# One scan loop over all 64 tiles: the next image's attention and first front inside the seventh tile

## The chip, the cores and the metric

One core of a Trainium2 chip runs the kernel. The metric is device time in microseconds (us) of one execution; the time before is the median of three runs.

## The reference, cut to what matters

The input `x` has 8 images of 512 channels and 64 x 64 positions. For each image two residual layers follow each other:

```
x = x + attention(_gn(x))      # group norm over 32 groups; Q, K from 4x4 means, V summed over 16 positions
x = x + ssm(_gn(x))            # group norm again, with moments of the new x
# attention: A = softmax(Q K^T / sqrt(512)), 256 x 256; out = repeat(A @ Vsum, 16)
# ssm: LayerNorm over 512 channels, cut in 4 chunks of 128; for each chunk
#   xi, z = in_proj; xc = silu(conv4(xi)); dt, B, C = x_proj(xc); dt = softplus(...)
#   h[t] = exp(dt*A) * h[t-1] + dt*xc*B   for 16 states and 256 inner channels;   y = sum over states of h*C
#   y = (y + xc*D) * silu(z); out_proj; + skip
# LayerNorm over 512 channels, 512 x 512 projection
```

The scan runs over all 4096 positions of an image, so its states and the convolution's last three columns go from tile to tile and start at zero in each image. The attention's output is needed before any position of the image can enter the second layer, and the second group norm needs the moments of the sum of both.

## The kernel before

An image is cut into 8 tiles of 512 positions (`T`), a tile into 4 **items** (one for each 128-channel chunk), an item into 16 **steps** (one for each state). A step is two scans on VectorE (DVE), one for each half of the 256 inner channels (`scan`, L921), with the decay `exp(dt*A)` written to PSUM by ScalarE (ACT, L649), the input product `u = dt*x*B` on DVE (11 of 16 steps, L901, `AHEAD` says in which step each is made) or on GpSimd (POOL, the 5 steps of `POOL_U`, L1187), the product with C on POOL (L1200) and the sum over states by an identity matmul on TensorE (PE, `state_sum`, L369). U, H and G are rings of four steps, so no engine can run more than four steps ahead of the one that frees a slot.

All five engines carry an order written out by hand. `window(tile, w)` emits the 16 steps of item `w` of a tile and, at fixed steps `s` in it, the **front** of item `w + 1`: the convolution as matmuls, its silu, the rows of B and C (stored and broadcast back by DMA from SyncE's queue, SP), and dt's softplus, which passes ACT, DVE (`dt_poly`, L938) and POOL (`dt_first`, `dt_sum`, `dt_x`, L1205 to L1214). `gate` (L927, step 2) waits until the state sums of the item before are complete. `j = w % 4` chooses what else lies in an item: the second LayerNorm of the tile before (j = 0), its projection and `finish` (j = 1, L957), the first LayerNorm of the next tile (j = 2) and the statistics of one slice of the *next image* (j = 3, `slice_moments`, `slice_rows`, `slice_blocks`). `late(j)` is 1 for j = 3 and moves the front one step back. The inner loop covers items 2 to 29 of an image as w = 2 to 5 of seven iterations.

Around it each image has a part of its own. On every engine `attention(b)` and `first_front` come first, alone, using the scan's own buffers (RING, ITEM, LV, LS, and DA, DTP, YP in PSUM); then windows 0 and 1, the loop, windows 2 and 3 of the last tile without a further front, and `last_end`, which ends the last tile.

## Time and profile before

| | |
|---|---|
| median of 3 runs | 17287.28 us (17285.9 to 17292.63) |
| the profiled execution's own time | 17281.15 us |
| its span, first to last instruction | 17279.2 us |
| DVE / POOL / PE / ACT busy, share of the span | 87% / 87% / 84% / 65% |
| mean granted TensorE clock | 0.931 |

The profile is of one execution; every row has its times. "Idle before, releaser" is the time an engine sat idle before a group of instructions and what ended it. In the 40 slices each digit is a busy share in tenths.

### The profile page before, as it was taken

What the parts mean: (1) busy time and instruction counts of PE and PEld (TensorE: products, weight loads), DVE (VectorE), ACT (ScalarE), POOL (GpSimd) and SP (SyncE); (2) the same over time, 40 slices, a digit from 0 to 9 for tenths busy, and PEclk for the clock granted to TensorE, in tenths of its full rate; (3) what the DMA queues carried; (4) which work ended last, traced back from release to release, by engine and by line L of the source; (5) the groups of instructions that cost most, each with busy time, mean ns of one, the idle gap of its engine ahead of it and who ended that gap; (6) DMA issues with size and microseconds to landing.
All of it is one profiled execution on the core that took longest, in us unless ns stands there. A gap on an engine that the chain in (4) does not pass through costs nothing. (4 is left out here: it accounts for less than half of the span.)

```text
span 17279.2 us, 159098 instructions
## 1 busy us (share of the span) xinstructions
PE 14535.6 (84%) x30720; PEld 5796.6 (34%) x30720; DVE 14988.9 (87%) x13132; ACT 11261.9 (65%) x18548; POOL 14970.7 (87%) x6268
## 2 busy tenths in 40 slices
PE   6888878888788887888878888788887888878888
PEld 2333333333333333333333333333333333333333
DVE  7999969999699996999969999699996999869998
ACT  4667657676566765667656666566665666656675
POOL 5999969999699996999969999699986999869998
PEclk8999989999899998999989999899998999989999
DMA  3444434444344443444434444344443444434443
GB/s 130 155 156 160 156 108 156 154 159 157 111 154 156 158 154 115 155 154 158 152 116 157 152 157 156 114 154 156 156 154 118 157 153 154 151 118 152 152 152 135
DMA packets 739059, 2535.91 MB, mean 147 GB/s; under 512 B 77240, under 2 KB 78016, under 8 KB 721728
## 3 DMA queue, kind: packets, MB, share of 16 engines
q1 hardware_dynamic: 738112, 2527.45, 42.8%
q14 instruction: 861, 7.05, 0.1%
q8 instruction: 86, 1.41, 0.0%
HBM read 2376.15 MB, written 150.99 MB: 146 GB/s over the span
## 5 line engine op out<-in xcount | busy, mean ns | idle before, releaser
L1200 POOL TENSOR_TENSOR RING<-RING,CS 128x1024 f32<-128x1024 f32 x4096 | 9832.9, 2419 | 1054.6 <-DVE RING L921 1037.3
L921 DVE TENSOR_TENSOR_SCAN RING<-DA,HS,RING 128x512 f32<-128x512 f32 x8192 | 9948.9, 1264 | 785.1 <-ACT DA L649 528.7
L369 PE MATMUL YP<-RING,EYE 128*128 128x512 f32 x16384 | 8378.6, 643 | 1931.3 <-POOL RING L1200 1899.3
L649 ACT ACTIVATE DA<-ITEM,AN 128x512 f32<-128x512 f32 x8192 | 5526.7, 685 | 3369.3 <-DVE RING L921 3359.7
L369 PEld LDWEIGHTS YP<-RING,EYE 128*128 128x128 f32 x16384 | 3122.7, 199 | 6731.5 <-issue 3495.4
L901 DVE TENSOR_TENSOR RING<-DTP,BS 128x1024 f32<-128x1024 f32 x2816 | 3374.9, 1206 | 0.2 <-DMA BS<-bc_rows 0.2
L1187 POOL TENSOR_TENSOR RING<-ITEM,BS 128x1024 f32<-128x1024 f32 x1280 | 3019.4, 2360 | 8.6
L369 PE MATMUL FL<-XN,WC 128*128 128x512 f32 x4096 | 1954.3, 622 | 48.1 <-ACT XN L734 36.6
L1205 POOL TENSOR_TENSOR ITEM<-ITEM,EX 128x1024 f32<-128x1024 f32 x256 | 602.6, 2354 | 1048.7 <-ACT EX L703 1048.7
L369 PEld LDWEIGHTS FL<-XN,WC 128*128 128x128 f32 x4096 | 847.4, 207 | 1194.5 <-issue 1151.3
L662 ACT ACTIVATE ITEM<-FL,COL 128x512 f32<-128x512 f32 x512 | 347.9, 680 | 1202.1 <-PE FL L369 1202.1
L369 PE MATMUL FL<-LS,WP 128*128 128x512 f32 x2048 | 978.4, 605 | 48.8 <-POOL LS L1218 48.8
L658 ACT ACTIVATE HS<-RING 128x2 f32<-128x2 f32 x4096 | 780.2, 190 | 12.3 <-DVE RING L921 12.3
L927 DVE TENSOR_TENSOR YZ<-ITEM,YP 128x1024 f32<-128x1024 f32 x256 | 311.0, 1215 | 535.6 <-PE YP L369 535.6
L369 PE MATMUL FL<-LS,MEAN 128*128 128x512 f32 x1024 | 561.7, 680 | 234.3 <-ACT LS L744 234.3
L938 DVE SCALAR_TENSOR_TENSOR YZ<-YZ,EM 128x1024 f32<-128x1024 f32 x256 | 519.8, 2030 | 233.8 <-ACT YZ L710 233.8
L369 PE MATMUL FL<-ROWS,WDT 8*128 8x512 f32 x1024 | 582.3, 648 | 50.5 <-ACT ROWS L675 15.9
L1210 POOL TENSOR_TENSOR ITEM<-ITEM,YZ 128x1024 f32<-128x1024 f32 x256 | 601.9, 2351 | 5.5 <-DVE YZ L938 4.9
L1214 POOL TENSOR_TENSOR ITEM<-ITEM 128x1024 f32<-128x1024 f32 x256 | 602.4, 2353 | 0.6
L369 PE MATMUL FL<-XN,WZ 128*128 128x512 f32 x1024 | 495.6, 606 | 126.9 <-ACT ITEM L662 126.9
L369 PEld LDWEIGHTS FL<-LS,WP 128*128 128x128 f32 x2048 | 391.2, 194 | 568.4 <-issue 567.5
L369 PE MATMUL FL<-YZ,WO 128*128 128x512 f32 x1024 | 507.0, 617 | 10.5 <-DVE YZ L927 10.5
(122 smaller groups left out, 10420.8 us busy)
## 6 DMA issues: line engine op xcount, KB each, us to landing
BS<-bc_rows SPq DMA_DIRECT2D x2048, 512.0 KB, 4.9
CS<-bc_rows SPq DMA_DIRECT2D x2048, 512.0 KB, 3.6
XR<-in_x SPq DMA_DIRECT2D x128, 1024.0 KB, 7.4
x_slices<-XR SPq DMA_DIRECT2D x64, 1024.0 KB, 8.0
XR<-x_slices SPq DMA_DIRECT2D x64, 1024.0 KB, 7.4
out<-XR SPq DMA_DIRECT2D x64, 1024.0 KB, 7.9
ITEM<-in_wqkv SPq DMA_DIRECT2D x24, 1024.0 KB, 5.5
bc_rows<-ROWS SPq DMA_DIRECT2D x256, 64.0 KB, 4.5
```

The source lines that it names most:

```text
L369: return pe.matmul(*a, **k)
L649: act.activation(DA[:, h, :], DT[:, i % 2, h, :], ACT.Exp, scale=AN[:, h, s:s + 1]).then_inc(dA_ready, 1)
L658: act.activation(HS[:, i % ITEMS, :, s:s + 1], H[:, slot(n), :, T - 1:T], ACT.Copy).then_inc(state_kept, 1)
L662: act.activation(XC[:, i % 2, h, :], FL[:, h, :], ACT.Identity, bias=CB[:, h:h + 1]).then_inc(xi_copied, 1)
L901: dve.tensor_tensor(U[:, slot(n)], DTP[:, :, :], BS[:, s % B_ROWS, :].unsqueeze(1).broadcast_to([P, NH, T]), ALU.mult).then_inc(u_dve, 1)
L921: dve.tensor_tensor_scan(H[:, slot(n), h, :], DA[:, h, :], U[:, slot(n), h, :], HS[:, i % ITEMS, h, s:s + 1], ALU.mult, ALU.add).then_inc( ...
L938: dve.scalar_tensor_tensor(out=YZ[:, :, :], in0=YZ[:, :, :], scalar=13.0 / 16, in1=EM[:, :, :], op0=ALU.add, op1=ALU.mult).then_inc(poly_r ...
L1187: pool.tensor_tensor(U[:, slot(n)], DTX[:, :, :], BS[:, s % B_ROWS, :].unsqueeze(1).broadcast_to([P, NH, T]), ALU.mult).then_inc(u_pool, 1)
L1200: pool.tensor_tensor(G[:, slot(n)], H[:, slot(n)], CS[:, s % C_ROWS, :].unsqueeze(1).broadcast_to([P, NH, T]), ALU.mult).then_inc(g_ready, 1)
L1205: pool.tensor_tensor(DT[:, i % 2], DT[:, i % 2], EX[:, :, :], ALU.add).then_inc(dt_begun, 1)
L1210: pool.tensor_tensor(DT[:, i % 2], DT[:, i % 2], YZ[:, :, :], ALU.add).then_inc(dt_ready, 1)
L1214: pool.tensor_tensor(DTX[:, :, :], DT[:, i % 2], XC[:, i % 2], ALU.mult).then_inc(dtx_ready, 1)
```

## The change

The image's own part goes. After one attention, one first front and windows 0 and 1 for image 0, one chain of windows runs through all 64 tiles. What image b + 1 needs is cut into pieces, and each piece has a step of a window of image b:

- Slices of statistics: one in w3 of tiles 0 to 3, two (w3 and w5) in tiles 4 and 5, none in tiles 6 and 7.
- In tile 6 (`coming=b + 1`): w2 has `aggregate`, the first group mean and variance; w3 the pooled inputs, the queries, keys and half of the values; w4 the other half, the scores and the exponentials; w5 the turned weights, the output O, its moments and the covariance. Projection 2 and 3 of w5 move back by up to one step.
- In w2 of tile 7 (`new=True`): the second variance, rstd and shift, and the front and first LayerNorm, one step later than elsewhere; its end (halo and first chunk) is in step 0 of w3 (`shifted`). ACT writes zeros in place of the kept states (`kept=False`) and of the halo.
- The results pass through the two front banks of PSUM (FP, LP) alone; Q, K, V and the weights A have buffers of their own; Wq and Wv are loaded into XT, Wk into XE, by SP's queue between its B and C rows. The norm of the pooled inputs moves from DVE to ACT (`pooled`, `summed`); the covariance is taken of the normed sums and divided back. In the beginning these loads come behind the statistics instead of ahead of them.

The diff, cut to its core (the pieces on the engines are the same operations as in the old `attention`, in halves):

```diff
+        QK = sb("QK", [P, 2, NCH, NB])
+        VS = sb("VS", [P, 2, CH])
+        AT = sb("AT", [P, 2, NB])
...
+        Q, K = QK[:, 0], QK[:, 1]
...
+        wt_flat, we_flat = (x.rearrange("p k t -> p (k t)") for x in (XT, XE))
+        WT, WE = (x.rearrange("p (k n) -> p k n", k=NCH) for x in (wt_flat, we_flat))
...
+            def load_wq(a):
+                sp.wait_ge(stats_done, a * NT + NT)
+                load_w(WT, 0, wq_loaded)
+            def load_wk(tile):
+                sp.wait_ge(stored, tile * 16)
+                load_w(WE, 1, wk_loaded)
+            def load_wv(a):
+                sp.wait_ge(q_ps, a * 2 + 2)
+                load_w(WT, 2, wv_loaded)
+            def load_end_after(t, tile, a):
+                sp.wait_ge(k_ps, a * 2 + 2)
...
+                if more:
+                    tile_step(b, 6, at, after_store=(b, 5), front=(b + 1, 0),
+                              extra={2: {0: lambda: load_wq(b + 1)},
+                                     3: {0: lambda: load_wk(at), 5: lambda: load_wv(b + 1)},
+                                     4: {1: lambda: load_end_after(6, at, b + 1)}})
+                    tile_step(b, 7, at + 1, after_store=(b, 6), front=(b + 1, 1))
...
+                    if new and s == 0:
+                        group_var(coming, 2)
...
+                            if new:
+                                pe.wait_ge(glog_ready, coming * 2 + 2)
+                            if j == 3 and coming is not None:
+                                pe.wait_ge(glog_ready, coming * 2 + 1)
...
+                        else:
+                            if s == 12:
+                                pe.wait_ge(final_ready, (ahead - 1) * NCH + 2)
+                                proj(2, (0, 1), low=True)
+                            if s == 13:
+                                proj(2, (2, 3), low=True)
+                            if s == 14:
+                                pe.wait_ge(final_ready, (ahead - 1) * NCH + 3)
+                                proj(3, (0, 1))
...
+                    if coming is not None and not new:
+                        if j == 2:
+                            if s == 9:
+                                front_left(tile, w + 1)
+                                group_mean(coming, 1)
+                            if s == 12:
+                                group_var(coming, 1)
+                        if j == 3:
+                            if s == 8:
+                                pe.wait_ge(yb_ready, tile * ITEMS + w)
+                                queries(coming, 0)
+                            if s == 9:
+                                front_left(tile, w + 1)
+                                queries(coming, 1)
+                            if s == 12:
+                                keys(coming, 0)
+                            if s == 13:
+                                keys(coming, 1)
+                            if s == 14:
+                                values(coming, 0)
+                            if s == 15:
+                                pe.wait_ge(k_ready, coming * 2 + 2)
+                        if j == 0:
+                            if s == 8:
+                                front_left(tile, w + 1)
+                                values(coming, 1)
+                            if s == 11:
+                                scores(coming)
+                            if s == 15:
+                                pe.wait_ge(prob_exp, coming + 1)
+                        if j == 1:
+                            if s == 8:
+                                front_left(tile, w + 1)
+                                turn(coming)
+                            if s == 10:
+                                attend(coming, 0)
+                            if s == 12:
+                                attend(coming, 1)
+                            if s == 15:
+                                group_mean(coming, 2)
...
+            with pe.Fori(0, BATCH - 1) as b:
+                with pe.Fori(0, NT - 2) as t:
                     for w in range(2, 2 + ITEMS):
                         window(b * NT + t, w)
-                window(b * NT + (NT - 1), 2, ln1=False)
-                window(b * NT + (NT - 1), 3, ln1=False, front=False)
-                last_end(b * NT + (NT - 1))
+                for w in range(2, 2 + ITEMS):
+                    window(b * NT + (NT - 2), w, coming=b + 1)
+                window(b * NT + (NT - 1), 2, new=True, coming=b + 1)
+                for w in range(3, 2 + ITEMS):
...
+            def keep_halo(new=False):
+                src = ZERO.unsqueeze(1).broadcast_to([P, NCH, HALO]) if new else XN[:, :, T:T + HALO]
...
+                    if coming is not None:
+                        if j == 1:
+                            if s == 0:
+                                prob_scale(coming)
+                            if s == 9:
+                                prob_turned(coming)
+                            if s == 11:
+                                attended(coming, 0)
+                            if s == 13:
+                                attended(coming, 1)
+                        if j == 2 and not new:
+                            if s == 14:
+                                group_rstd(coming, 1)
+                        if j == 2 and new and s == 1:
+                            group_rstd(coming, 2)
+                        if j == 3:
+                            if s == 2:
+                                pooled(coming)
+                            if s == 7:
+                                summed(coming)
+                            if s == 11:
+                                head(Q, BQ, q_ps, q_ready, coming, 0)
+                            if s == 12:
+                                head(Q, BQ, q_ps, q_ready, coming, 1)
+                            if s == 13:
+                                head(K, BK, k_ps, k_ready, coming, 0)
+                            if s == 15:
+                                head(K, BK, k_ps, k_ready, coming, 1)
+                        if j == 0:
+                            if s == 0:
+                                value_copy(coming, 0)
+                            if s == 10:
+                                value_copy(coming, 1)
+                            if s == 14:
+                                prob(coming)
...
+            def summed(a):
+                act.wait_ge(coef_ready, a * 2 + 2)
+                for k in range(NCH):
+                    last = act.activation(XS[:, k], XS[:, k], ACT.Identity, bias=GSH16[:, k:k + 1],
+                                          scale=GRS[:, k:k + 1])
+                last.then_inc(xs_norm, 1)
...
+                    if coming is not None:
+                        if j == 2 and not new:
+                            if s == 5:
+                                aggregate(coming)
+                            if s == 11:
+                                deviation(coming, 1)
+                            if s == 15:
+                                first_shift(coming)
+                        if j == 0:
+                            if s == 13:
+                                score_max(coming)
+                            if s == 15:
+                                score_sum(coming)
+                        if j == 1:
+                            if s == 12:
+                                o_moments(coming, 0)
+                            if s == 14:
+                                o_moments(coming, 1)
+                            if s == 15:
+                                covariance(coming)
+                        if j == 2 and new:
+                            if s == 0:
+                                deviation(coming, 2)
+                            if s == 2:
+                                second_shift(coming)
...
+            def deviation(a, n):
+                mean, var, first = (GMS[:, :], MV[:, :, 1], 1) if n == 1 else (M1[:, :], V1[:, :], 7)
+                dve.wait_ge(gmean_ready, a * 2 + n)
+                dve.tensor_copy(GMN[:, :], FP[:, 0:NCH]).then_inc(gmean_kept, 1)
+                dve.wait_ge(gmean_kept, a * 2 + n)
+                dve.tensor_tensor(DEV[:, :], mean, GMN[:, :], ALU.subtract).then_inc(chain, 1)
+                link(a, first + 1)
+                dve.tensor_tensor(GSQ[:, :], DEV[:, :], DEV[:, :], ALU.mult).then_inc(chain, 1)
+                link(a, first + 2)
+                dve.tensor_tensor(GVAR[:, :], GSQ[:, :], var, ALU.add).then_inc(dev_ready, 1)
+            def first_shift(a):
+                dve.wait_ge(grstd_ready, a * 2 + 1)
+                dve.tensor_scalar(GRS16[:, :], GRS[:, :], 1.0 / SS, None, ALU.mult).then_inc(coef_ready, 1)
+                dve.scalar_tensor_tensor(out=GSH[:, :], in0=GMN[:, :], scalar=-1.0, in1=GRS[:, :],
+                                         op0=ALU.mult, op1=ALU.mult).then_inc(gshift_ready, 1)
...
+            def covariance(a):
+                dve.wait_ge(o_aggr, a + 1)
+                dve.wait_ge(score_ps, a + 1)
+                dve.wait_ge(xs_norm, a + 1)
                 for k in range(NCH):
...
+                    last = dve.scalar_tensor_tensor(out=OXP[:, k, :].rearrange("p (t n) -> p t n", t=NT),
+                                                    in0=O[:, k, :].rearrange("p (t n) -> p t n", t=NT),
+                                                    scalar=OV[:, k, 0:1], in1=XS[:, k],
+                                                    op0=ALU.subtract, op1=ALU.mult)
+                last.then_inc(chain, 1)
+                link(a, 4)
                 dve.tensor_reduce(COV[:, :], OXP[:, :, :], AX_X, ALU.add).then_inc(cov_ready, 1)
+                dve.wait_ge(cov_ready, a + 1)
+                dve.tensor_tensor(COV[:, :], COV[:, :], RGR[:, :], ALU.mult).then_inc(chain, 1)
                 dve.tensor_tensor(M1[:, :], MV[:, :, 0], OV[:, :, 0], ALU.add).then_inc(chain, 1)
-                dve.wait_ge(cov_ready, b + 1)
-                dve.scalar_tensor_tensor(out=V1[:, :], in0=COV[:, :], scalar=2.0 / NB, in1=MV[:, :, 1],
+                link(a, 6)
+                dve.scalar_tensor_tensor(out=V1[:, :], in0=COV[:, :], scalar=2.0 / (NB * SS), in1=MV[:, :, 1],
                                          op0=ALU.mult, op1=ALU.add).then_inc(chain, 1)
-                links[0] += 1
-                link()
+                link(a, 7)
                 dve.tensor_tensor(V1[:, :], V1[:, :], OV[:, :, 1], ALU.add).then_inc(moments_ready, 1)
-                dve.wait_ge(moments_ready, b + 1)
-                group_moments(2, M1[:, :], V1[:, :], A2[:, :], C2[:, :])
-                assert links[0] == CHAIN
+                dve.wait_ge(moments_ready, a + 1)
...
+            with dve.Fori(0, BATCH - 1) as b:
+                with dve.Fori(0, 4) as t:
                     for w in range(2, 2 + ITEMS):
-                        window(b * NT + t, w, t, image=coming)
-                window(b * NT + (NT - 1), 2, NT - 1, ln1=False)
-                window(b * NT + (NT - 1), 3, NT - 1, image=coming, ln1=False, front=False)
-                last_end(b * NT + (NT - 1))
-
-                dve.wait_ge(g_summed, (b + 1) * (NT * STEPS))
-                dve.wait_ge(state_kept, (b + 1) * (NT * STEPS))
-                dve.wait_ge(scanned, (b + 1) * (2 * NT * STEPS))
-                dve.wait_ge(final_ready, (b + 1) * (NT * NCH))
```

## Rows read from the trace of the kernel before

**Rows 1.** The page: busy times, and the busy tenths in 40 slices
```profile
PE 14535.6 (84%) x30720; PEld 5796.6 (34%) x30720; DVE 14988.9 (87%) x13132; ACT 11261.9 (65%) x18548; POOL 14970.7 (87%) x6268
...
DVE  7999969999699996999969999699996999869998
```

**Rows 2.** First and last start of the attention's addition to an image's tile 0
```profile
L1106 DVE TENSOR_TENSOR XR<-XR,O x8: 2291/2292/2293, 117.6 to 15188.2; 128x2048 f32<-128x2048 f32 x8
```

**Rows 3.** The same addition to tiles 2 to 7 of image 0, once a tile
```profile
L1224 POOL TENSOR_TENSOR XR<-XR,O x6: 3675/3689/3730, 559.7 to 1815.1; 128x2048 f32<-128x2048 f32 x6
```

**Rows 4.** Busy time and granted clock of a steady tile and of a boundary
```profile
core 0: us, PE busy (x) PEld busy (x) DVE busy (x) ACT busy (x) POOL busy (x), PEclk, DMA share, GB/s
936.20:1187.90 251.70, 219.77 (x465) 86.50 (x465) 231.67 (x198) 174.62 (x287) 234.51 (x99) 0.95 0.45 156
2171.80:2335.90 164.10, 100.60 (x244) 51.10 (x244) 29.64 (x65) 41.34 (x60) 16.37 (x8) 0.81 0.15 52
```

**Rows 5.** Timeline of DVE across the first boundary
```profile
2169.34 2.43 DVE L921 TENSOR_TENSOR_SCAN RING<-DA,HS,RING 128x512 f32<-128x512 f32 x2
...
2271.55 2.29 DVE L1106 TENSOR_TENSOR XR<-XR,O 128x2048 f32<-128x2048 f32 x1
...
2335.91 4.81 DVE L921 TENSOR_TENSOR_SCAN RING<-DA,HS,RING 128x512 f32<-128x512 f32 x4 [9.65 <-POOL RING L1187]
```

**Rows 6.** Waits in four steady tiles (1000 to 2004 us): total, times, longest
```profile
POOL RING L1200 <- DVE RING L921: 64.9, 41, 3.3
DVE RING L921 <- ACT DA L649: 37.9, 38, 2.2
DVE YZ L927 <- PE YP L369: 30.1, 12, 3.9
```

**Rows 7.** Timeline of PE in the first boundary: the attention's matmuls
```profile
2227.91 9.49 PE L369 MATMUL DA<-RING,ITEM 128*128 128x256 f32 x32 [4.07 <-DVE RING L1053]
2237.24 7.07 PE L369 MATMUL YP<-RING,ITEM 128*128 128x256 f32 x32
2244.14 3.60 PE L369 MATMUL FL<-ITEM,RING 128*128 128x512 f32 x8
2247.57 3.62 PE L369 MATMUL DTP<-LV 128*128 128x256 f32 x16
...
2256.32 3.69 PE L369 MATMUL YP<-LS 128*128 128x256 f32 x16 [1.26 <-ACT LS L833]
```

**Rows 8.** Groups of instructions in the first boundary's attention (2220 to 2272 us)
```profile
L823 ACT ACTIVATE LV<-YP,COL 128x256 f32<-128x256 f32 x4 | 1.6, 475 | 5.3 <-PE YP L369 5.3
...
L1072 DVE BATCH_NORM_STATS2 SO<-O 128x6 f32<-128x256 f32 x4 | 1.4, 412 | 7.6 <-ACT O L836 7.6
...
L1091 DVE TENSOR_REDUCE SM<-RING 128x4 f32<-128x1024 f32 x1 | 1.2, 1220 | 0.0
...
L1040 DVE BATCH_NORM_AGGREGATE SM<-ST 128x2 f32<-128x48 f32 x4 | 1.0, 324 | 0.0
...
L833 ACT ACTIVATE LS<-DA 128x512 f32<-128x512 f32 x1 | 0.6, 591 | 0.0
...
L1020 DVE TENSOR_TENSOR SM<-SM 128x4 f32<-128x4 f32 x2 | 0.3, 162 | 0.1
```

**Rows 9.** Timeline of POOL, item 19's `dt_first` and the C product behind it
```profile
1413.54 2.35 POOL L1205 TENSOR_TENSOR ITEM<-ITEM,EX 128x1024 f32<-128x1024 f32 x1
1415.84 3.33 POOL L1200 TENSOR_TENSOR RING<-RING,CS 128x1024 f32<-128x1024 f32 x1
```

**Rows 10.** Timeline of DVE: `dt_poly` (two inputs in SBUF) in two neighbouring items
```profile
1414.54 2.42 DVE L938 SCALAR_TENSOR_TENSOR YZ<-YZ,EM 128x1024 f32<-128x1024 f32 x1
...
1473.39 1.19 DVE L938 SCALAR_TENSOR_TENSOR YZ<-YZ,EM 128x1024 f32<-128x1024 f32 x1
```

**Rows 11.** Timeline of DVE in the prologue: the fourth slice's statistics
```profile
31.33 1.29 DVE L963 BATCH_NORM_STATS2 ST<-XR 128x6 f32<-128x512 f32 x2 [6.24 <-DMA XR<-in_x]
```

**Rows 12.** The addition to tiles 2 to 7 of image 7, which has no statistics
```profile
L1224 POOL TENSOR_TENSOR XR<-XR,O x6: 3672/3696/3737, 15629.1 to 16880.5; 128x2048 f32<-128x2048 f32 x6
```

**Rows 13.** Waits of SP's queue in four steady tiles (1000 to 2004 us)
```profile
SPq L268 <- POOL RING L1200: 864.6, 128, 11.4
```

More of the change, by code:

```diff
@@ L454, in xi_second, with window @@
                 xi_half(tile, w + 1, 1)
-            def window(tile, w, first=False, front=True, ln1=True, ln2=True):
+            def window(tile, w, first=False, front=True, ln1=True, ln2=True, new=False, coming=None):
                 j = w % ITEMS
-                d = late(j)
+                d = late(j, new)
                 ahead = tile + w // ITEMS
@@ new lines, in values @@
+            def values(a, m):
+                if m == 0:
+                    pe.wait_ge(wv_loaded, a * 16 + 16)
+                    pe.wait_ge(xs_norm, a + 1)
+                    pe.wait_ge(k_ready, a * 2 + 1)
+                for k in range(NCH):
+                    last = mm((LP, FP)[m][:, :], XS[:, k, m * (NT // 2):(m + 1) * (NT // 2), :].rearrange("p t n -> p (t n)"), WT[:, k, :],
+                              start=(k == 0), stop=(k == NCH - 1))
+                last.then_inc(v_ps, 1)
@@ L806, in window @@
                         if s == 0:
+                            if shifted:
+                                keep_halo(new=True)
+                                apply_norm(ahead + 2, (0,))
                             apply_norm(ahead + 2, (1,))
@@ new lines, in attended, with attention @@
+            def attended(a, h):
+                act.wait_ge(o_ps, a * 2 + h + 1)
+                for o in (2 * h, 2 * h + 1):
+                    last = act.activation(O[:, o, :], FP[:, o % 2 * NB:(o % 2 + 1) * NB], ACT.Identity, bias=BV16[:, o:o + 1])
+                last.then_inc(o_ready, 1)
+            def attention():
+                group_rstd(0, 1)
+                pooled(0)
+                head(Q, BQ, q_ps, q_ready, 0, 0)
+                head(Q, BQ, q_ps, q_ready, 0, 1)
+                summed(0)
+                head(K, BK, k_ps, k_ready, 0, 0)
+                head(K, BK, k_ps, k_ready, 0, 1)
+                value_copy(0, 0)
+                value_copy(0, 1)
+                prob(0)
+                prob_scale(0)
+                prob_turned(0)
+                attended(0, 0)
+                attended(0, 1)
+                group_rstd(0, 2)
@@ L977, in slice_blocks, with window @@
                                   ALU.add).then_inc(stats_done, 1)
-            def window(tile, w, t, image=None, first=False, front=True, ln1=True, ln2=True):
+            def window(tile, w, stat=None, first=False, front=True, ln1=True, ln2=True, new=False, coming=None):
                 j = w % ITEMS
-                d = late(j)
+                d = late(j, new)
                 ahead = tile + w // ITEMS
```

622 lines of the change are left out of this document (338 added, 284 removed).

## The prediction

> **What bounds the kernel now.** I read the page first. PE, DVE and POOL are each busy for over four fifths of the span, and in the slices the lines of DVE and POOL fall together every fifth or sixth slice: eight images, seven boundaries at which everything stops [rows 1]. The windows put numbers on it. A steady tile has DVE and POOL busy for 231.7 and 234.5 of 251.7 us; the 164.1 us between the last scan of image 0 and the first of image 1 have POOL at work for 16.4 us and DVE for 29.6 [rows 4, 5]. So two things matter: how long a boundary is, and what a steady tile has to spare for the same work.
>
> The period of an image is (15188.2 - 117.6) / 7 = 2152.9 us [rows 2]. The period of a steady tile is (1815.1 - 559.7) / 5 = 251.1 us [rows 3]. Eight such tiles are 2008.6 us, so a boundary costs 144.3 us net: less than 164.1, because an image's first and last items lack some of the work and are short.
>
> In the steady tile no single engine is the bound. The waits of four tiles show a ring of three: POOL waits for scans for 64.9 us, DVE waits at the gate for the state sums (which follow POOL's products) for 30.1 us and for ACT's decays for 37.9 us [rows 6]. Within an item I read this as two stretches. From the gate to about step 10 DVE sets the pace, with ACT close behind it, and POOL idles. From there, where dt's three products and the u products of the next item come on top, POOL sets it until the next gate, where DVE waits up to 3.9 us. DVE work added in the first stretch costs its whole length, in the second nothing until it exceeds that wait.
>
> **The sum without the moved work.** 17279.2 - 7 x 144.3 = 16269 us of span. Prologue and end stay, but for the weights: 3 MB of loads no longer stand ahead of the fourth slice, where DVE waited 6.2 us [rows 11]. The prologue's attention, now through two PSUM banks, with its hand-overs in a row, takes some 5 us more by my walk. That makes -1: 16268.
>
> **The moved work, X us for each boundary.** The raw amounts: PE 9.5 + 7.1 + 3.6 + 3.6 (the second half of the values, the same) + 3.6 + 3.7 = 31 us and some 3 for the small ones [rows 7]; ACT some 28 instructions at 0.2 to 0.6 us, 14 us; DVE 10 us, by the durations of the same or the nearest operations [rows 8]. What of it lies on the path:
>
> (a) `aggregate` at step 5 of w2, in DVE's own stretch: four aggregations, a memset and a copy, 1.5 us, all of it.
>
> (b) ACT. Queries, keys, O and probabilities are copied in steps in which ACT waits for scans anyway (3.3 us or so behind every light step); nothing. `summed` (4 x 0.475 = 1.9 us) comes at step 7 beside the softplus, where ACT is full, as do `prob_turned` and `value_copy` (0.6 each): 1.5 + 0.6 + 0.6 = 2.7 us. If the cover were gone it would be 14.
>
> (c) The end of w5 and the start of the new w2. PE has 251.7 - 219.8 = 31.9 us idle in a tile [rows 4], just what it gets. In w3 and w4 I walked the order with PE's times: the queries fall where PE has caught up, the keys and values into its waits for POOL, and the state sum before the gate comes when POOL is done; nothing. In w5 PE is full: `attend` and the delayed projection 3 make `finish(3)` some 4 us late on DVE. Behind it on DVE comes the covariance (four passes at 0.4, a reduction of 1.2, four small ones at 0.16: 3.5), then the deviation (0.9) and the second shift (0.3), with the scans of the new item queued behind them. To these come the waits for POOL of part (d): 2.8, 1.8 and 0.7. The front one step later adds 1.7. The gate's wait of 3.9 is used up: 4 + 3.5 + 0.9 + 0.3 + 5.3 + 1.7 - 3.9 = 11.8 us.
>
> (d) A wait that the boundary did not have. `dt_poly` takes 1.19 us when no POOL product runs as it starts, but 2.42 us when it starts 1.0 us after `dt_first`: it ends 1.1 us after `dt_first` does, and the C product behind takes 3.33 us, where 2.35 is usual [rows 9, 10]. So a DVE instruction with two inputs in SBUF stands behind a running POOL product, and POOL's next one behind it. The change puts 16 such instructions beside a busy POOL: three in each deviation, one in each shift, eight in the covariance. Before, POOL was idle for all of them and a small one took 0.16 us. Those in a chain of waits can each meet a new product. For the first deviation and shift (steps 11 and 15 of w2, POOL's stretch) that is up to 4 x 2.35 = 9.4, of which the slack before the gate takes about half: 4 us. At the end of w5 POOL runs dry while DVE is held, so the later ones go free: the 5.3 us in (c). From both sides: nothing, and 16 x 2.35 = 37.6 us.
>
> The Trainium skill (SBUF — State Buffer, Who interferes with whom) says it as a rule: a VectorE instruction with two SBUF inputs and a GpSimd instruction that reads SBUF exclude each other for their whole length. By that rule the trace agrees for `dt_poly`, to 0.1 us; read at its strictest, with a whole product for every one of the 16, it gives the port rival below.
>
> (e) Statistics: two more in w5 of tiles 4 and 5, where DVE has the `finish` steps as well, none in w3 of tiles 6 and 7. The last image has none at all, yet its tile period is (16880.5 - 15629.1) / 5 = 250.3 us [rows 12], so they cost 0.8 us where they stand. In w5 their first part, 2.5 us at step 3 (two of its four passes take 1.29 us [rows 11]), may not be hidden. +3 - 1 = 2 us; between -1 and 7.
>
> X = 1.5 + 2.7 + 11.8 + 4 + 2 = 22 us. 16268 + 7 x 22 = 16422 us of span. The profiled execution's own time is 2 us above its span and the median of the runs 6 us above that: **16430 us**, 5.0% less.
>
> **Rivals.** *All is hidden.* DVE and POOL each have 17 to 20 us idle in a tile, and the slack at the gate swallows the pieces. Only (a) and a little are left, X = 3: 16268 + 21 + 8 = 16297. For it: removing the statistics from the last image's tiles bought next to nothing. Against: DVE's stretch has no slack, and the covariance stands before scans that nothing has computed ahead.
>
> *The port.* Each of the 16 instructions waits a whole product: 37.6 us in place of the 9.3 that I have in (c) and (d), X = 50: 16626. For it: the links between them are semaphores, so POOL's next product starts in between. Against: at the end of w5 POOL must itself wait for the scan.
>
> *The hand-overs are exposed.* PE's 34, ACT's 14 and DVE's 10 us each come on top, since the engines wait for each other in turn as at the boundary, X = 60: 16268 + 420 + 8 = 16696. For it: PE has no spare in sum. Against: its pieces lie in different items, and it waits for POOL for much of its idle time.
>
> *Slower.* X has to exceed 144 us. The one mechanism that reaches so far is SP's queue: the loads of Wk, Wv and of the end tile wait there for `stored`, `q_ps` and `k_ps`, and behind each stand the C and B rows of the next steps, for which POOL, DVE and PE wait, PE being who must raise `q_ps`. It decides when such a wait holds the rows for over 40 us in three items. Now SP waits for POOL for 6.8 us on average before each C load (864.6 / 128) [rows 13], so it has that much in hand, and by my walk `q_ps` holds it for 4 us.
>
> *It still drains*, if one piece can't start before the scan of the image is over: X near 144, no change. The order has no such wait.
>
> **Chances.** Forecast (X from 12 to 34, 16360 to 16514) 0.66; all hidden 0.12; port 0.12; exposed 0.07; slower 0.02; no change 0.01. The range takes in the port and, but for its lowest edge, the hidden case: 16300 to 16640. About 0.2% (35 us) either way is what a measurement of this kernel can tell from no change. Faster 0.97, same 0.01, slower 0.02.
>
> **What the profile of the changed kernel would show.** The slices of DVE and POOL stay at 9 throughout, without the seven dips, and DVE is busy for about 91%. Where the additions to tiles 1 to 7 of an image follow each other, the tile period is 251 us; from a boundary tile's w2 to the next tile's w3 some 20 us are added, most at the end of w5, where DVE waits for PE before `finish(3)`. The small DVE instructions of the deviation show waits behind POOL's products, the covariance's four passes over 0.4 us each. PE's granted clock is at 0.95 or above everywhere. I am wrong if the steady tile itself changes (1 us is 62 us), if ACT waits long for PE at the heads of w3, or if C rows come late in tile 6.

## The result, and the profile after

Before: 17286.89 us, the median of 4 runs (17285.9 to 17292.63). After: 16606.22 us, the median of 4 runs (16604.51 to 16619.53). The ratio is 0.9607, with a 95% interval from 0.9591 to 0.9624: 3.9% less time, where 5.0% less was forecast. The time lies in the range on record, 16300 to 16640, but above the forecast case's own range (16360 to 16514); it is 20 us from the time that the port rival gave.

The page of the changed kernel: busy times, and the tenths in 40 slices.

```profile
span 16603.5 us, 158027 instructions
...
PE 14390.7 (87%) x30720; PEld 5782.7 (35%) x30720; DVE 15104.1 (91%) x13023; ACT 11266.2 (68%) x18635; POOL 15002.7 (90%) x6275
...
DVE  6999999999999999999999999999999999998988
...
PEclk9999999999999999999999999999999999999999
```

The seven dips of [rows 1] are gone and DVE is at 91%, as forecast. The span gives X by the prediction's own sum: (16603.5 - 16268) / 7 = 47.9 us for each boundary, where 22 was forecast. So the drain, 144.3 us, is gone, and what lies on the path in its place is twice the forecast.

Where it lies shows in the lengths of the items. The table gives the time from an item's first scan (DVE, L1148) to the next item's, as a mean over images 0 to 6; the first column is the mean of the same item in tiles 2 to 5 of the kernel before. It is worked out from the scans' start times. The last five columns are kernels of the experiments below.

| item | before | after | second slice in w4 (run 1) | moments at step 13 (run 5) | reduction for copy (run 2) | port-free (run 3) | port-free and moments (run 11) |
|---|---|---|---|---|---|---|---|
| tile 5, w4 (that of tile 4 is within 0.5) | 60.8 | 60.9 | 67.1 | 60.4 | 61.1 | 61.4 | 60.9 |
| tile 4, w5 (a second slice) | 63.5 | 73.2 | 62.2 | 68.5 | 72.2 | 72.7 | 68.5 |
| tile 5, w5 (a second slice) | 63.5 | 70.6 | 61.6 | 68.2 | 71.3 | 72.1 | 68.2 |
| tile 6, w2 | 63.5 | 77.6 | 79.1 | 71.2 | 70.5 | 63.6 | 64.4 |
| tile 6, w3 | 62.9 | 61.4 | 61.1 | 61.5 | 61.5 | 59.5 | 60.8 |
| tile 6, w4 | 60.8 | 63.8 | 63.8 | 63.8 | 63.8 | 63.8 | 63.8 |
| tile 6, w5 | 63.5 | 74.6 | 74.9 | 74.8 | 74.8 | 74.7 | 74.7 |
| tile 7, new w2 | 63.5 | 72.7 | 73.2 | 73.1 | 72.8 | 67.9 | 67.7 |
| tile 7, w3 | 62.9 | 61.3 | 61.1 | 60.7 | 61.3 | 61.7 | 61.7 |
| all 32 items of an image | | 2055.8 | 2053.0 | 2042.1 | 2049.6 | 2036.3 | 2029.5 |

Five items carry the loss. The two with a second slice of statistics are 9.7 and 7.1 us longer than before. The w2 in which the next image's mean and variance are made is 14.1 longer, and the two in which attention ends and the new image's tile 0 begins are 11.1 and 9.2 longer. All other items of an image together are within 2 us of before, though w4 of tile 6 is 3.0 longer and the w3 of tiles 6 and 7, which hold no statistics any more, are 1.5 and 1.6 shorter; the steady tile is unchanged.

The first of them, DVE at the aggregation and GpSimd (POOL) beside it, in the timelines of the changed kernel:

```profile
1833.56 0.76 DVE L1275 BATCH_NORM_AGGREGATE SM<-ST 128x2 f32<-128x48 f32 x3
1834.36 5.87 DVE L1278 COPY SM<-SM 128x4 f32<-128x4 f32 x1
1840.60 2.46 DVE L1148 TENSOR_TENSOR_SCAN RING<-DA,HS,RING 128x512 f32<-128x512 f32 x2 [0.37 <-DVE SM L1278]
```

```profile
1833.23 2.39 POOL L1467 TENSOR_TENSOR RING<-RING,CS 128x1024 f32<-128x1024 f32 x1
1835.53 2.38 POOL L1454 TENSOR_TENSOR RING<-ITEM,BS 128x1024 f32<-128x1024 f32 x1
1837.83 2.37 POOL L1467 TENSOR_TENSOR RING<-RING,CS 128x1024 f32<-128x1024 f32 x1
1843.14 2.36 POOL L1467 TENSOR_TENSOR RING<-RING,CS 128x1024 f32<-128x1024 f32 x1 [2.93 <-DVE RING L1148]
```

A copy of four columns, with one input, takes 5.87 us. It ends at 1840.23, and the third POOL product that overlaps it ends at 1840.20. After it POOL idles for 2.93 us, since the scans were held too. Over the whole execution the same copy takes 0.17 us once, in the prologue with POOL idle, and 5.8 to 5.9 us seven times:

```profile
L1278 DVE COPY SM<-SM x8: 170/5854/5873, 61.4 to 14177.0; 128x4 f32<-128x4 f32 x8
```

The Trainium skill (SBUF — State Buffer, Who interferes with whom) names copies and `tensor_scalar`s among the instructions that can take the port pair shared with GpSimd, and says that a reduction on trn2 never does. The prediction drew on that section for two-input instructions alone.

The first deviation and the first shift (DVE, w2 of tile 6) in the same timeline:

```profile
1865.97 0.93 DVE L1286 TENSOR_TENSOR SM<-SM 128x4 f32<-128x4 f32 x1
1866.94 2.26 DVE L1288 TENSOR_TENSOR SM<-SM 128x4 f32<-128x4 f32 x1
1869.24 2.26 DVE L1290 TENSOR_TENSOR SM<-SM 128x4 f32<-128x4 f32 x1
...
1885.98 0.71 DVE L1294 TENSOR_SCALAR SM<-SM 128x4 f32<-128x4 f32 x1
1886.61 0.15 DVE L1295 SCALAR_TENSOR_TENSOR SM<-SM 128x4 f32<-128x4 f32 x1
1886.79 2.21 DVE L1298 TENSOR_SCALAR SM<-SM 128x4 f32<-128x4 f32 x1
```

An instruction of this size took 0.16 us before [rows 8]. Here a link of the chain ends with a POOL product, and the next link meets a new one, so that it takes 2.26 us. Both `tensor_scalar`s, with one input, wait as well. The instruction between them (L1295) takes 0.15 us here and in one other image, and 2.4 in the other five.

The end of w5 and the start of the new w2, on DVE and then on POOL:

```profile
2054.05 6.12 DVE L1165 SCALAR_TENSOR_TENSOR YZ<-YZ,EM 128x1024 f32<-128x1024 f32 x1
...
2080.62 0.75 DVE L1184 SCALAR_TENSOR_TENSOR XR<-FL,COL,XR 128x512 f32<-128x512 f32 x1 [2.01 <-PE FL L388]
2081.29 4.53 DVE L1336 SCALAR_TENSOR_TENSOR QK<-O,SM,XS 128x256 f32<-128x256 f32 x4
2085.85 1.22 DVE L1342 TENSOR_REDUCE SM<-QK 128x4 f32<-128x1024 f32 x1
...
2090.67 2.35 DVE L1286 TENSOR_TENSOR SM<-SM 128x4 f32<-128x4 f32 x1
2093.06 3.60 DVE L1288 TENSOR_TENSOR SM<-SM 128x4 f32<-128x4 f32 x1
2096.69 0.16 DVE L1290 TENSOR_TENSOR SM<-SM 128x4 f32<-128x4 f32 x1
```

```profile
2082.22 2.52 POOL L1467 TENSOR_TENSOR RING<-RING,CS 128x1024 f32<-128x1024 f32 x1
2090.66 2.34 POOL L1467 TENSOR_TENSOR RING<-RING,CS 128x1024 f32<-128x1024 f32 x1 [5.92 <-DVE RING L1148]
2092.96 3.68 POOL L1493 TENSOR_TENSOR XR<-XR,O 128x2048 f32<-128x2048 f32 x1
```

`finish(3)` (L1184) waits for PE, here for 2.0 us, and the covariance's four passes (L1336) take 4.53 us, two of them in turn with POOL's last products. This first boundary isn't the usual one: in the other six the wait is 3.71 us, near the 4 forecast, and only the first pass waits (the four take 3.0 us in five images, 4.13 in one). Then POOL runs dry and idles 5.92 us, as forecast, and the four small instructions behind the covariance are free. Not so the second deviation: the one scan in between starts a POOL product, and behind that product POOL has the 3.68 us attention addition ready, which L1288 waits through (3.60 us).

w4 of tile 6 is 3.0 longer for another reason. Here are the windows of w4 in tile 4 and in tile 6, with PE's busy time behind the length and the granted clock as the third figure from the end, and the gate's wait for PE in the second:

```profile
1426.50:1486.95 60.45, 52.11 (x117) 20.80 (x116) 55.61 (x49) 43.67 (x72) 57.24 (x26) 1.00 0.51 175
1949.65:2013.50 63.85, 63.72 (x155) 28.38 (x154) 56.66 (x53) 45.37 (x78) 57.76 (x26) 1.00 0.44 149
```

```profile
1964.97 1.22 DVE L1154 TENSOR_TENSOR YZ<-ITEM,YP 128x1024 f32<-128x1024 f32 x1 [4.82 <-PE YP L388]
```

PE is busy for 63.72 of 63.85 us at a granted clock of 1.00, and the gate waits 4.82 us for it, where 2.2 to 3.9 are usual at that place.

### The profile page after: what moved, and what is told of

It is laid out like the page before. It is cut to its first block and busy times, and to the rows that moved or that the text cites. A ratio compares the mean times of both kernels' runs of the same rounds, so it can differ in the third digit from the quotient of the medians.

```text
span 16603.5 us, 158027 instructions
## 1 busy us (share of the span) xinstructions
PE 14390.7 (87%) x30720; PEld 5782.7 (35%) x30720; DVE 15104.1 (91%) x13023; ACT 11266.2 (68%) x18635; POOL 15002.7 (90%) x6275
## 5 line engine op out<-in xcount | busy, mean ns | idle before, releaser
L1148 DVE TENSOR_TENSOR_SCAN RING<-DA,HS,RING 128x512 f32<-128x512 f32 x8192 | 9955.4, 1264 | 811.0 <-ACT DA L777 614.1
L388 PE MATMUL YP<-RING,EYE 128*128 128x512 f32 x16384 | 8293.4, 638 | 1648.6 <-POOL RING L1467 1578.7
L787 ACT ACTIVATE HS<-RING 128x2 f32<-128x2 f32 x3648 | 694.9, 190 | 1.5 <-DVE RING L1148 1.5
L1477 POOL TENSOR_TENSOR ITEM<-ITEM,YZ 128x1024 f32<-128x1024 f32 x256 | 601.8, 2351 | 11.1 <-DVE YZ L1165 11.1
```

The source lines that it names most:

```text
L388: return pe.matmul(*a, **k)
L787: act.activation(HS[:, i % ITEMS, :, s:s + 1], src, ACT.Copy).then_inc(state_kept, 1)
L1148: dve.tensor_tensor_scan(H[:, slot(n), h, :], DA[:, h, :], U[:, slot(n), h, :], HS[:, i % ITEMS, h, s:s + 1], ALU.mult, ALU.add).then_inc( ...
L1477: pool.tensor_tensor(DT[:, i % 2], DT[:, i % 2], YZ[:, :, :], ALU.add).then_inc(dt_ready, 1)
```

## The experiments

Unless a run says otherwise, the changed kernel's 16606.22 us is what it is compared with. A kernel's own five runs spread over some 10 to 30 us, so a difference under 15 us is called none.

**1. The second slice of statistics in w4.** In place of w5, for tiles 4 and 5:

```
-  stat=... else (b + 1, t + t - 3) if w == 5 else None
+  stat=... else (b + 1, t + t - 3) if w == 4 else None
```

> The second statistics slice of tiles 4 and 5 is taken in item w4, with no projection in it, in place of w5. My theory: its 5 us of VectorE work come in w5 ahead of steps that projection and finish already fill, which cost 16 us per image (w5 of tiles 4 and 5 took 72.4 and 70.2 us where 63.3 is usual); in w4, where VectorE runs a light item, it costs at most 3 us. 10 to 13 us less for each of 7 images, 70 to 90 us in all: 16515 to 16535 us. Rival: the work costs its VectorE time wherever it stands; then w4 grows by what w5 loses, and the time stays within 20 us of the changed kernel's 16606.

Measured: 16587.91 us, 18 less. w5 is back to 62.2 and 61.6 us, but w4 went from 61 to 67. So the rival holds, at its edge of 20 us: a second slice costs as much as its DVE work (some 6 us: 2.4 + 2.3 + 0.7 + 1.0) in w4, and by the lengths of the items some 2 us more than that in w5 (18 / 14 = 1.3 by the whole time). My account of what is special in w5 was wrong.

**2. A reduction in place of the copy.**

```
-  dve.tensor_copy(GMS[:, :], MV[:, :, 0])
+  dve.tensor_reduce(GMS[:, :], MV[:, :, 0:1], AX_X, ALU.add)
```

> The 128x4 copy of the group means (5.9 us in the first image of the changed kernel, 0.17 us in its prologue, where GpSimd is idle) becomes a reduction over one element, which writes the same four numbers by another kind of instruction. My theory: the copy is held by GpSimd's products at the SBUF port, a reduction isn't; it takes under 0.3 us, item w2 of tile 6 gets 4 to 6 us shorter, and 7 times that is 28 to 42 us: 16564 to 16578. Rival: the copy waits for the aggregation before it, or for the write to land, and the reduction takes as long: no change, 16606 within 15 us.

Measured: 16566.58 us, 40 less. All eight reductions take 0.157 us, also the seven that lie wholly within a POOL product:

```profile
L1278 DVE TENSOR_REDUCE SM<-SM x8: 157/157/158, 61.3 to 14141.7; 128x4 f32<-128x4 f32 x8
```

w2 of tile 6 is 7.1 us shorter. By the Trainium skill's rule on reductions (the same section), the trace agrees. The 5.7 us were a wait for POOL, and all of it was on the path.

**3. Port-free deviation and coefficients.** The reduction of run 2, and

```
+  dev, sq = FP[:, 8:8 + NCH], FP[:, 16:16 + NCH]
-  dve.tensor_tensor(DEV[:, :], mean, GMN[:, :], ALU.subtract)
-  dve.tensor_tensor(GSQ[:, :], DEV[:, :], DEV[:, :], ALU.mult)
-  dve.tensor_tensor(GVAR[:, :], GSQ[:, :], var, ALU.add)
+  dve.tensor_tensor(dev, mean, FP[:, 0:NCH], ALU.subtract)
+  dve.tensor_tensor(DEV[:, :], mean, FP[:, 0:NCH], ALU.subtract)
+  dve.tensor_tensor(sq, DEV[:, :], dev, ALU.mult)
+  dve.tensor_tensor(GVAR[:, :], sq, var, ALU.add)
```

with GRS16 and GSH16 made by two ACT instructions in `pooled`.

> As the run with the reduction, and the deviation reads the group mean from PSUM and keeps its deviation and its square there, so that each of its instructions has at most one input in SBUF (one small instruction more); the two scaled coefficients are made by ScalarE. In the covariance and the two shifts nothing changes. My theory: waits for GpSimd's products make up most of what w2 of tile 6 is longer (13 to 15 us per image), and part of it at the start of the new w2. w2 of tile 6 gets 10 to 12 us shorter, the rest 0 to 5 us: 70 to 120 us in all, 16485 to 16535. Rival: what is longer there comes from the aggregation (1.5 us) and from TensorE, which must finish group_mean and group_var between its other work: then only the 4 to 6 us of the copy go, 16565 to 16580, and this run is like the one with the reduction alone.

Measured: 16470.58 us, 136 less, more than expected. The chain in the timeline of this kernel:

```profile
1864.52 0.17 DVE L1290 TENSOR_TENSOR FL<-SM,FL 128x4 f32<-128x4 f32 x1
1864.60 0.15 DVE L1291 TENSOR_TENSOR SM<-SM,FL 128x4 f32<-128x4 f32 x1
1864.78 0.17 DVE L1293 TENSOR_TENSOR FL<-SM,FL 128x4 f32<-128x4 f32 x1
1864.98 0.16 DVE L1295 TENSOR_TENSOR SM<-FL,SM 128x4 f32<-128x4 f32 x1
```

Four instructions in 0.6 us where three took 5.5; they take as long in all 14 places, each beside a running POOL product. w2 of tile 6 is at 63.6, what a w2 took before; the w3 behind it gains 1.9 and the new w2 4.8. Beyond run 2 that is 6.9 + 2.0 + 4.9 = 13.8 us for each boundary.

**4. Thin attention.** Queries, keys, values and scores with `for k in range(1)` for `range(NCH)`.

> This kernel leaves out three of the four products over the channels in the queries, keys, values and scores: 20.5 of the 27.4 us that they take on TensorE at each boundary. In the prologue, where nothing hides them, some 15 to 20 us go by either theory. My theory: TensorE does this work while it would wait for GpSimd, so that each boundary gets 0 to 2 us shorter: 15 to 35 us in all, 16571 to 16591. Rival (TensorE is the bound, the work is exposed): 20 us for each of 7 boundaries besides the prologue, 155 to 165 us less: 16441 to 16451.

Measured: 16577.91 us, 28 less. The first scan starts at 165.6 us where it was 178.5, so 13 are the prologue's; that leaves 15 for seven boundaries, 2 each. My theory holds, at its edge: PE does nearly all of this work in time that it has. The items say where it doesn't: w4 of tile 6 is 61.4 us long where it was 63.8, and no other item from w2 of tile 6 to w3 of tile 7 moves by more than 0.5. There PE is now busy for 57.71 of 61.71 us, and the gate waits 2.90 for it in place of 4.82:

```profile
1942.63:2004.34 61.71, 57.71 (x129) 23.83 (x128) 56.65 (x52) 45.36 (x78) 57.78 (x26) 0.97 0.43 155
```

```profile
1955.82 1.22 DVE L1154 TENSOR_TENSOR YZ<-ITEM,YP 128x1024 f32<-128x1024 f32 x1 [2.90 <-PE YP L388]
```

**5. The moment passes at step 13 of w5**, in place of step 3; the rest of the slice stays at steps 12 and 14. (The edit is cut: the wait for the slice's load stands ahead of step 12 too.)

```
-  if s == 3:
+  if s == (13 if j == 1 else 3):
       slice_moments(t, XT)
```

> In w5 of tiles 4 and 5 the four moment passes of the second slice (2.4 us of VectorE) stand at step 13 in place of step 3; nothing else moves. My theory, after the run with the second slice in w4: VectorE work between the gate and step 10 costs its whole length and in w5 more, since TensorE, delayed there, has projections to catch up with (its state sum of step 4 came 5.6 us later for 2.4 us of VectorE work); at step 13, where GpSimd sets the pace, it costs 0 to 2 us. Each of the 14 items gets 3 to 5 us shorter: 16535 to 16565. Rival: the item's total of VectorE work decides, wherever in the item it stands: no change, 16606 within 15 us.

Measured: 16508.24 us, 98 less, more than expected. The same 2.4 us of work, moved by ten steps within its item, take 4.7 and 2.4 us off the two w5 items. That refutes the rival, which run 1 had favoured: where in the item the work stands does matter. Almost as large a part, 6.4 us, comes off where nothing was changed, w2 of tile 6:

```profile
1829.18 0.24 DVE L1280 COPY SM<-SM 128x4 f32<-128x4 f32 x1
```

The copy now meets POOL at the very end of a product (1827.05 + 2.35 = 1829.40) and is in after 0.24 us, seven times of seven. So a change in one item also moves the phase of what follows: against POOL's products the copy starts at another moment.

**6. The aggregation at step 8**, in place of step 5.

> The aggregation with its 128x4 copy stands at step 8 of w2 in tile 6 in place of step 5. At step 5 GpSimd has products waiting and runs them back to back, and the copy waited 5.9 us, over two whole products; at step 8 it idles 0.9 us in the run with the port-free instructions. My theory: a waiting VectorE instruction gets the port only when GpSimd's queue has a gap, so that here the copy takes 0.2 to 2.4 us: 3.5 to 5.5 us less for each of 7 images, 16567 to 16582. Rival: the length of the wait has nothing to do with a backlog (it is a fixed cost beside a busy GpSimd): the copy takes 5 to 6 us at step 8 too, and the time stays within 15 us of 16606.

Measured: 16564.93 us, 41 less; w2 of tile 6 is 5.4 shorter.

```profile
1851.07 0.17 DVE L1278 COPY SM<-SM 128x4 f32<-128x4 f32 x1
```

POOL's last product ended at 1850.77, so that the copy met an idle POOL. The wait is no fixed cost of working beside POOL. That a gap is needed, as my theory has it, isn't borne out: in run 5 the copy went in with POOL's next product right behind it (at 1829.36), and so did the links of the first deviation.

**7. The copy made twice** at step 5.

```
+  dve.tensor_copy(GSQ[:, :], MV[:, :, 0])
   dve.tensor_copy(GMS[:, :], MV[:, :, 0])
```

> The aggregation's 128x4 copy, at step 5 of w2 in tile 6, is made twice, into two places. My theory: the first waits until GpSimd's queue of ready products is empty, 5.8 us; when it is let in, GpSimd has nothing ready, and the second goes in the same gap, 0.2 us: 0 to 3 us more in all, 16606 to 16609. Rival: each such copy pays a wait of its own: 2.4 us (one product) or 5.8 us each, 17 to 41 us more, 16623 to 16647.

Measured: 16607.02 us, no difference.

```profile
1835.24 5.89 DVE L1278 COPY SM<-SM 128x4 f32<-128x4 f32 x1
1841.05 0.15 DVE L1279 COPY SM<-SM 128x4 f32<-128x4 f32 x1
1841.57 1.28 DVE L1148 TENSOR_TENSOR_SCAN RING<-DA,HS,RING 128x512 f32<-128x512 f32 x1 [0.37 <-DVE SM L1279]
```

The second copy is free: POOL has nothing ready by then. The cost is in the place, not in the number of instructions there.

**8. A thin covariance.** `for k in range(1)` in its multiplying passes.

> This kernel leaves out three of the four multiplying passes of the covariance, 0.86 us each on average, at the end of w5 of tile 7. My theory: VectorE is what all wait for there, so that w5 gets 2 to 3.4 us shorter at each of 7 boundaries and the prologue 1.2: 15 to 25 us less in all, 16581 to 16591. Rival (the passes lie beside GpSimd's and TensorE's own arrears, and TensorE, which runs 7 us late there, sets the end): 0 to 3 us in all, 16603 to 16606.

Measured: 16600.41 us, 6 less, inside the spread: nearer to the rival. The items tell more than the time does: w5 of tile 6 is 73.4 us long, where it is 74.5 to 74.9 in all the other kernels, so the three passes cost their own length there (3 x 0.4 = 1.2 us) and nothing beyond. The timelines of DVE and POOL tell why it isn't the 2 to 3.4 of my theory.

```profile
2084.33 0.75 DVE L1184 SCALAR_TENSOR_TENSOR XR<-FL,COL,XR 128x512 f32<-128x512 f32 x1 [3.71 <-PE FL L388]
2085.00 1.85 DVE L1336 SCALAR_TENSOR_TENSOR QK<-O,SM,XS 128x256 f32<-128x256 f32 x1
2086.88 1.22 DVE L1342 TENSOR_REDUCE SM<-QK 128x4 f32<-128x1024 f32 x1
```

```profile
2084.23 2.34 POOL L1467 TENSOR_TENSOR RING<-RING,CS 128x1024 f32<-128x1024 f32 x1
2091.70 2.35 POOL L1467 TENSOR_TENSOR RING<-RING,CS 128x1024 f32<-128x1024 f32 x1 [5.13 <-DVE RING L1148]
```

The one pass that is left waits until POOL's last ready product ends at 2086.57, and is done 0.3 us later: the wait stays, whether one pass follows or four.

**9. The covariance ahead of `finish(3)`.**

```
+  if s == 15 and o == 3 and coming is not None:
+      covariance(coming)
   ... finish(o, ahead - 1, low=coming is not None)
...
-  if s == 15:
-      covariance(coming)
```

> At step 15 of w5 in tile 7 the covariance stands before finish(3), which there waits 2.0 us for TensorE's projection, in place of behind it. My theory: the wait is filled with covariance work, 2 us less at each of 7 boundaries: 14 us less, 16592. Rival: the next scan is held by something later than finish(3), TensorE or GpSimd, and nothing changes; or the covariance now starts while GpSimd still runs its last products and waits for them at the port, 2 to 5 us each time, and the time is 10 to 30 us longer.

Measured: 16603.12 us, no difference.

```profile
2083.08 7.07 DVE L1336 SCALAR_TENSOR_TENSOR QK<-O,SM,XS 128x256 f32<-128x256 f32 x4
```

```profile
2084.47 2.53 POOL L1454 TENSOR_TENSOR RING<-ITEM,BS 128x1024 f32<-128x1024 f32 x1
2086.95 2.52 POOL L1467 TENSOR_TENSOR RING<-RING,CS 128x1024 f32<-128x1024 f32 x1
2095.30 2.34 POOL L1467 TENSOR_TENSOR RING<-RING,CS 128x1024 f32<-128x1024 f32 x1 [5.83 <-DVE RING L1148]
```

The passes start sooner and take 7.07 us where they took 4.53: three of them now end with a POOL product each (at 2084.5, 2087.0 and 2089.5), and the fourth goes free. The wait of 2.0 us (3.7 in most images) that was filled is given to the port, and w5 of tile 6 stays at 74.7 us. So the time that `finish(3)` waits for PE in the changed kernel costs nothing by itself.

**10. Half of attention's output** left out: `attend` over one of the two halves of keys.

> This kernel leaves out half of the products of attention's output, 1.8 us of TensorE in w5 of tile 7. My theory after the covariance runs: what ends late there is GpSimd's arrears of products, behind which the covariance's first pass must wait, whatever comes before it on VectorE or TensorE; so nothing changes, 16600 to 16606 (0 to 6 us less in all). Rival (the prediction's account: attention and the delayed projection make finish(3) late, and that time is exposed): 1.8 us less at each of 7 boundaries and 1.8 in the prologue, 12 to 15 us less, 16591 to 16594.

Measured: 16609.2 us, no difference, and w5 of tile 6 is 74.8. PE's work there is not exposed. Of my theory, runs 8 to 10 bear out its outcome, but not its wording: run 9 shows passes being let in between two products.

**11. Port-free and moments at step 13 together.**

> The port-free aggregation, deviation and coefficients together with the moment passes of the second slices at step 13 of w5. My theory: the two costs lie in different items and add up, 136 and 98 us less: 16365 to 16385. Rival: each takes up slack at a gate that the other needs too, and 30 to 50 us of it are lost: 16400 to 16425.

Measured: 16422.28 us (16406.67 to 16423.44), 184 less than the changed kernel, and the fastest kernel of this study; against the kernel before the ratio is 0.9499, from 0.9486 to 0.9512. The rival's number, but not its cause. 50 us of the sum of both are missing, and the table shows where: by themselves, run 5 takes 6.4 us off w2 of tile 6 and run 3 takes 14.0, but together they take 13.2, 7.2 less than the sum, and 7 x 7.2 = 50 us. The copy's wait can be saved only once.

**12. All moment passes late**: as run 11, and in w3 at step 11 in place of step 3.

> As the run with both, and in w3 the moment passes of the first slice stand at step 11 in place of step 3, between their two reductions. My theory: VectorE work between the gate and step 10 costs its length, so that these 42 places give 0.5 to 2 us each: 20 to 80 us less than the run with both. Rival: the statistics in w3 are hidden (tiles without them have a period only 0.8 us shorter), and at step 11, with both reductions close by, they fill GpSimd's stretch too: the time is the same or up to 40 us longer.

Measured: 16531.24 us, 109 more than run 11. The six w3 items of an image that hold a slice are 0.9 to 2.9 us longer, 11 us together, and the w5 items two behind them 7 together. The rival's direction holds, and by more than it gave: what was right in w5 is wrong in w3, where a reduction at step 9 and two at step 12 already stand around it. Which engine's wait it is there was not followed further.

## Why the prediction came out as it did

The mechanism was right in the main: the drain of 144.3 us went, 96.4 of it for good, and nothing starves for rows. The time lies in the range on record because that range took in the port rival; it is 92 us above the forecast case's own. The base of the sum held: the steady tile is as it was, and the first scan starts at 178.5 us where it was 182.1, 3.6 sooner where 1 was forecast. What was off is X, 47.9 for 22. By its terms:

- **(a) The aggregation, 1.5 us: off by the copy.** By the trace it takes its own 1.5 and 5.7 of waiting; run 2 took off 40 us, 5.7 a boundary. The step that failed is the list of 16 instructions, "with two inputs in SBUF". Copies and `tensor_scalar`s belonged on it, here three more on the path: L1278, L1294 and L1298.
- **(d) The port in w2, 4 us: too low by half.** The chains take 0.93 + 2.26 + 2.26 and on average 0.7 + 1.7 + 2.2 us, 10.1 together, some 1 of it their own: near the bound of 9.4 on record. I took half of it as covered by the slack before the gate. Run 3 gives back 6.9 + 2.0 = 8.9 beyond run 2: nothing was covered. As I read it, DVE's wait at the gate exists when POOL is late; a DVE that waits for POOL in POOL's stretch holds the scans that POOL needs next, so POOL idles (3.60 us behind the first deviation) and the slack goes with it.
- **(e) Statistics, 2 us between -1 and 7: measured 14.6**, as 9.7 and 7.1 in the two w5 items less 1.8 and 0.4 in the two items behind the first. The row that I went by, the 0.8 us that they cost in w3 [rows 3, 12], holds for w3 alone; the same work costs 6 in w4 (run 1) and more in w5. Run 5 locates 7.1 of it in the first part at step 3, which was the doubt on record ("may not be hidden"), for which 3 us had been put in.
- **(b) and (c) ACT, PE in w3 and w4, and the end of w5 with the new w2, 14.5 us: measured 21.7** (3.0 + 11.1 + 9.2 - 1.6 in tile 6's w4 and the three items behind it). The 3.0 in w4 are a term that was put at nothing: "the state sum before the gate comes when POOL is done". PE is full there and the gate waits for it; the thin attention of run 4 takes 2.4 of the 3.0 away. ACT's 2.7 no run separates. Of the rest, 4.9 are the second deviation's wait (run 3), where 1.8 had been put down; the prediction had overlooked POOL's attention addition, the 3.68 us behind its next product. PE's lateness at `finish(3)` (4 us) is there, 3.71 in most images, but adding it to the covariance (3.5 us) was wrong: with the covariance in its place in run 9 nothing changes. The first pass ends when POOL's ready products do, whatever comes before it, and of the four passes three cost their 1.2 us behind it (run 8).

These terms add up to 7.2 + 8.9 + 14.6 + 21.7 = 52.4 us, 4.5 more than the 47.9: w3 of tile 6 is in none of them, and in run 3, without the waits, it is 3.4 shorter than before (59.5 for 62.9).

So the port rival's time came about from half of its mechanism. Port waits on the path make up 5.7 + 8.9 + 4.9 = 19.5 us of the 47.9, not 37.6, and statistics another 14.6. Why w5 of tile 6 as a whole is 11.1 us longer isn't settled. `dt_poly`'s wait in it explains little: 6.1 us (2.4 is usual) in six images, but in image 1, the second, it takes 1.20 us, 4.9 less, and w5 is 73.5 us long there where the others are 74.6 to 74.9, so that it costs about 1.3. The covariance's passes are 1.2. What is left fits POOL's arrears: in this item POOL starts 28 instructions where w5 of tile 3 has 25, since the covariance's first pass waits until POOL has run dry, and three of them are 7 us. That is read from the trace; no run tested it.

The other rivals: the SP queue kept up (from tile 6's w2 to the new w2 of image 0 POOL's waits are for DVE, 51 us, and once for PE, none for a row), and run 4, which leaves out 20.5 us of PE's work in w3 and w4 at each boundary, gains 2 us there, so that little of it is exposed. The granted clock was a little under the 0.95 forecast, 0.94 in the steady tiles and 0.90 in the new w2:

```profile
559.70:1815.10 1255.40, 1096.94 (x2300) 432.06 (x2301) 1160.94 (x996) 864.51 (x1422) 1163.37 (x487) 0.94 0.47 156
...
2088.10:2161.00 72.90, 59.14 (x125) 23.24 (x124) 67.21 (x56) 48.81 (x81) 56.11 (x24) 0.90 0.37 121
```

## What to carry to other kernels

When small instructions are moved from a stretch where GpSimd is idle to one where it is busy, list every VectorE instruction that can want the shared port, copies and `tensor_scalar`s with one input too, and price each link of a chain at one whole GpSimd product; then write them so that they don't want it: a reduction for a copy, an operand in PSUM, a scaled copy on ScalarE. A cost read off in one item of a software pipeline doesn't carry to another: the same 6 us of statistics cost 0.8 in w3, 6 in w4 and 7 to 10 in w5, and moving the moment passes late saved 98 us in w5 and lost 109 in w3. When several delays meet before the same hand-over, don't add them: ask which is last, and what the ones before it only wait for. And look at every boundary, not at the first: here the first one is unlike the other six.

## What the runs showed of the hardware

A waiting VectorE instruction is usually let in when the running GpSimd product ends, though GpSimd's next one is ready (2.26 and 2.26 us in the deviation, three times 1.7 to 2.6 in the covariance of run 9). But not always: the copy at step 5 waited over two such ends for the third, in seven images of seven, and 9 of the 256 `dt_poly`s of the changed kernel took as long, six of them in w5 of tile 6, the longest 6.24 us:

```profile
L1165 DVE SCALAR_TENSOR_TENSOR YZ<-YZ,EM x256: 1196/2413/6241, 167.6 to 16483.0; 128x1024 f32<-128x1024 f32 x128
```

The kernel before has four of that length. The copy got in only when POOL had nothing ready any more, as in run 7. Products overlap or follow each other by the same few hundredths of a microsecond in both cases, and what decides between them stays open; no run was made for it. Runs 5 and 6 show only that a start at another moment avoids it.
